# The MLP's first projection in 11 tiles instead of 12: gates and values of the last 64 units share one tile

## The chip, the cores and the metric

The kernel runs on one core of a Trainium2 chip. The core has a matrix engine (TensorE, PE in the rows, with its weight loads as PEld), three engines for elementwise work (VectorE or DVE, ScalarE or ACT, GpSimd or POOL), a queue that issues DMAs (SyncE or SP), an on-chip memory of 128 partitions and PSUM, eight banks of 128 partitions by 512 fp32 numbers into which TensorE writes. The metric is the device time of one execution in microseconds (us); lower is better. Before: 1258.32 us, the median of 3 runs (1258.1 to 1260.74).

## The reference, cut to what matters

A decoder block in fp32 on x of shape (4, 512, 256): causal self-attention with 16 heads, cross-attention with 16 heads of 16, and a network of two layers of local attention and a gated MLP. Each sub-block adds its result to x. The change touches the MLP alone, which runs for 2 layers and 4 batches, eight times:

```python
h = shift_token(x)                                   # half the channels moved one token on
h = (h - mean) / sqrt(var + 1e-05) * lg + lb
h = h @ w1 + b1                                      # (512, 256) @ (256, 1364)
a, g = jnp.split(h, 2, axis=-1)                      # values and gates, 682 each
h = a * jax.nn.gelu(g, approximate=False)
x = x + h @ w2 + b2                                  # (512, 682) @ (682, 256)
```

## The kernel before, in words

Every engine has its own list of instructions, written out in order, and waits on semaphores. The first half of the time is self-attention (a loop over 32 pairs of heads) and cross-attention. Then come eight steps, m = 0 to 7, one for a layer and a batch (layer m // 4, batch m % 4). A step has tokens to q, k, v (`qkv_tile`), rotation and norms, four pairs of heads of local attention (scores `Sa` and `Sb`, softmax, transposes `Ta` and `Tb`, weighted values `AV`), an output projection (`wo`), and the MLP: `stats`, `norm`, `apply`, `hnT` (the normed tokens transposed), the first projection `hid0` to `hid5` and the second `w20` and `w21`.

The steps overlap. Four strings (`STEP_PE`, `STEP_DVE`, `STEP_ACT`, `STEP_POOL`, lines 312 to 325) say in which order each engine goes through one cycle; `hid5@-1` there is the last tile of the MLP of the step before, `hT@2` the transposes of y for the step after the next. Items whose step doesn't exist (m over 7) drop out. The last items, from `closing` (line 376) on, are in an order of their own, with the MLP of step 7 at the very end.

The MLP's 682 hidden units are cut into NF = 6 tiles: five of FT = 114 and one of FL = 112. For a tile f TensorE makes first the gates (`w1g`) and then the values (`w1a`), each into a PSUM bank of its own, [units, 512 tokens], as a product of six matmuls: two halves of the 256 channels, and for each three terms, since weights and tokens are split into a rounded part and a rest (`w1_hi`, `w1_lo`, `hnT_hi`, `hnT_lo`) (`hidden_part`, line 1797; the instructions are recorded under line 1461 in the helper `product`). ScalarE applies GELU with the gate's bias to the gates and writes `gl` (`gates`, L950). VectorE adds the value's bias to the values, multiplies with `gl` and writes `hid` (`hidden`, L1388). The second projection (`second_part`, line 1810) takes for each half of the tokens 12 products of 256 columns, which TensorE runs as 24 instructions, with the units of a tile as the contracted dimension. It waits until VectorE has read the values of the last three tiles.

PSUM banks 2, 5, 6 and 7 (class "g") go round among q, k, v, the projections, the shifted half and the weighted values, in the order of TensorE's list (`turn`, line 395): a product waits until the bank's user four turns before has been read. In the trace all of these are called psum, both weight parts w, and q, k, v's weights wqkv.

Around the last tile TensorE's order is: transposes `Ta2`, `hid5`, `v3` (the last v tile of the next step), `hT`, `w20`. On ScalarE it is `hid4 Ta2 hid5`, then rounded weights (once), `hT` and the exponentials `eb3`. On VectorE `hid4 Ta2 hid5`, then `hT`.

Of the kernel before, what the change touches and what calls it, by code (L numbers as in the profile page):

```python
# [27 lines left out]
NF = 6  # L28
FT = -(-HID // NF)
FL = HID - FT * (NF - 1)  # L30
W = 128
# [50 lines left out]
def build(nc, a, out, x2_dram):  # L82

    with ExitStack() as ctx:
        def sem(name):
            return ctx.enter_context(nc.semaphore(name))

        def sbt(stack, name, shape, dt=F32):
            return stack.enter_context(nc.sbuf_tensor(name, shape, dt))
# [87 lines left out]
        w1_hi = sbt(ctx, "w1_hi", [P, E2, 2 * HID], F32R)  # L177
        w2 = sbt(ctx, "w2", [FT, NF, D])
        wo = sbt(ctx, "wo", [P, FPAIRS, D])
        lng = sbt(ctx, "lng", [P, DEPTH, E2])  # L180
        lnb = sbt(ctx, "lnb", [P, DEPTH, E2])
        b1 = sbt(ctx, "b1", [FT, DEPTH, 2, NF])
        b2 = sbt(ctx, "b2", [P, D])
# [11 lines left out]
        gl = sbt(ctx, "gl", [P, GELU_T, S])  # L195
        hid = sbt(ctx, "hid", [FT, NF, S])

# [56 lines left out]
        ld_shift = sem("ld_shift")  # L254
        w_hi, w_lo = sem("w_hi"), sem("w_lo")
        w1_hi_ok, w1_lo_ok = sem("w1_hi_ok"), sem("w1_lo_ok")
        hn_hi, hn_lo = sem("hn_hi"), sem("hn_lo")
# [141 lines left out]
        for what, *at in pe_order:  # L399
# [18 lines left out]
            if what == "w1":  # L418
                turn(("w1g", *at), "g")
                turn(("w1a", *at), "g")  # L420
            if what == "sh":
# [26 lines left out]
        def wait_read(eng, use):  # L448

            bank, n = use  # L450
            eng.wait_ge(read[bank], n + 1)
# [5 lines left out]
        def wait_early(eng):  # L457

            wait_full(eng, plan["KV", B - 1])
            wait_full(eng, plan["x1T", B - 1, 1])  # L460

        def frows(f):
            return FT if f < NF - 1 else FL

# [14 lines left out]
        def _(sp):  # L479
# [28 lines left out]
            def layer_w2(l):  # L508
                main = a["w2"][l, 0:FT * (NF - 1), :].rearrange("(k p) c -> p k c", p=FT)
                sp.dma_start(w2[:, 0:NF - 1, :], main).then_inc(ld_w2, 16)  # L510
                sp.dma_start(w2[0:FL, NF - 1, :], a["w2"][l, FT * (NF - 1):HID, :]).then_inc(ld_w2, 16)

# [90 lines left out]
        def _(pool):  # L603
# [67 lines left out]
            def rotate_k(m, t):  # L671
# [10 lines left out]
                pool.tensor_tensor(k3, k3, r, ALU.mult).then_inc(l_k, 1)  # L682

            def mlp_rstd(m):

                pool.wait_ge(f_mv, T * (m + 1))
                pool.tensor_scalar(rstd[:, 0, :], mv[:, 0, :, 1], LN_EPS, None, ALU.add).then_inc(f_eps, 1)
                pool.wait_ge(f_eps, m + 1)
                pool.tensor_tensor(rstd[:, 0, :], rstd[:, 0, :], neg_half[:, 0:T], ALU.pow).then_inc(f_rstd, 1)
# [53 lines left out]
        def _(act):  # L743
# [200 lines left out]
            def gates(m, f):  # L944
                use = plan["w1g", m, f]
                bank = wait_full(act, use)
                if f >= GELU_T:
                    wait_read(act, plan["w1a", m, f - GELU_T])
                rows = frows(f)
                act.activation(gl[0:rows, f % GELU_T, :], bank[0:rows, :], ACT.Gelu,  # L950
                               bias=b1[0:rows, m // B, 1, f:f + 1]).then_inc(read[use[0]], 1)

# [38 lines left out]
        def _(dve):  # L991
# [390 lines left out]
            def hidden(m, f):  # L1382

                use = plan["w1a", m, f]
                wait_read(dve, plan["w1g", m, f])
                bank = wait_full(dve, use)
                rows = frows(f)
                dve.scalar_tensor_tensor(hid[0:rows, f, :], bank[0:rows, :], b1[0:rows, m // B, 0, f:f + 1],  # L1388
                                         gl[0:rows, f % GELU_T, :], ALU.add, ALU.mult).then_inc(read[use[0]], 1)

# [64 lines left out]
        def _(pe):  # L1455
# [341 lines left out]
            def hidden_part(m, f):  # L1797
                if f == 0:
                    pe.wait_ge(hn_lo, E2 * (m + 1))
                    if m % B == 0:  # L1800
                        pe.wait_ge(w1_lo_ok, E2 * (m // B + 1))
                rows = frows(f)
                for what, lo in (("w1g", HID + f * FT), ("w1a", f * FT)):
                    use = plan[what, m, f]
                    bank = wait_free(pe, use)
                    product(bank[0:rows, :], [(w[:, e, lo:lo + rows], h[:, e, :]) for e in range(E2)
                                              for w, h in ((w1_hi, hnT_lo), (w1_lo, hnT_hi), (w1_hi, hnT_hi))])\
                        .then_inc(full[use[0]], 1)

            def second_part(m, tp):  # L1810
                for f in range(NF - 3, NF):
                    wait_read(pe, plan["w1a", m, f])
                if m % B == 0:
                    pe.wait_ge(ld_w2, 32 * (m // B + 1))
                use = plan["w2", m, tp]
                bank = wait_free(pe, use)
                for i in range(2):
                    t = 2 * tp + i
                    ins = product(bank[:, i * D:(i + 1) * D],
                                  [(hid[0:frows(f), f, t * P:(t + 1) * P], w2[0:frows(f), f, :]) for f in range(NF)])  # L1820
                ins.then_inc(full[use[0]], 1)
# [88 lines left out]
```

## Time and profile before

| | before |
|---|---|
| median of 3 runs | 1258.32 us (1258.1 to 1260.74) |
| the profiled execution | 1258.88 us |
| its span, first to last instruction | 1257.1 us |
| mean granted TensorE clock | 0.986 |
| TensorE busy | 1168.3 us (93%) |
| VectorE busy | 840.2 us (67%) |
| ScalarE busy | 686.9 us (55%) |
| GpSimd busy | 587.9 us (47%) |

The durations of TensorE's instructions overlap: one starts while the one before it still drains. Busy time is the time covered by at least one of them, and the time that an instruction adds to a row of them is the distance from start to start. A line of a chain of waits gives start, length and what ran, with the number of instructions; in it, the times follow each other without a gap. In the rows of a timeline, brackets give the idle time ahead of the instruction and what ended it.

### The profile page before, as it was taken

How to read it: one execution, taken by the hardware profiler on the slowest of the kernel's cores; microseconds unless marked ns; L12 is line 12 of the kernel's file. 1: busy time of each engine (PE TensorE's matmuls, PEld its weight loads, DVE VectorE, ACT ScalarE, POOL GpSimd, SP SyncE). 2: the span in 40 equal slices, each digit the busy share in tenths (PEclk: the TensorE clock that was granted, in tenths of full speed). 3: DMA queues.
4: the chain of work that ended last, by engine and by line, in shares of the span. 5: the costliest groups of instructions: out<-in, count | busy, mean ns of one | idle time of the engine just before them, and what ended most of it. 6: DMA issues, size and time to landing. Idle time of an engine off the chain costs nothing.

```text
span 1257.1 us, 20486 instructions
## 1 busy us (share of the span) xinstructions
PE 1168.3 (93%) x6672; PEld 893.2 (71%) x6672; DVE 840.2 (67%) x2443; ACT 686.9 (55%) x1696; POOL 587.9 (47%) x648
## 2 busy tenths in 40 slices
PE   5899999999999899986689999999999999999888
PEld 4677777777777666755467787777877778777666
DVE  7677777778777365588688657667675776755331
ACT  3667667577676034162366746647465565654721
POOL 2344454444544211147677556564655646563430
PEclk9899999999999999998799999999999999999999
DMA  7112122121223210014000000000001000010010
GB/s 226 44 42 76 35 50 72 38 50 34 51 51 109 77 34 1 1 59 159 1 2 1 1 1 18 1 2 1 1 18 45 28 2 1 2 64 4 1 51 17
DMA packets 31628, 46.11 MB, mean 37 GB/s; under 512 B 4572, under 2 KB 19632, under 8 KB 31536
## 3 DMA queue, kind: packets, MB, share of 16 engines
q1 hardware_dynamic: 31536, 44.98, 12.6%
q8 instruction: 45, 0.74, 0.3%
q14 instruction: 47, 0.39, 0.1%
HBM read 24.00 MB, written 4.19 MB: 22 GB/s over the span
## 4 chain that ended last, share of the span: by engine, by line
PE 53%; issue 20%; POOL 15%; DVE 7%; ACT 4%; DMA 0%; POOLq 0%; DVEq 0%; ACTq 0%
PE psum L1461 33%; POOL probs L625 13%; PE psum L1721 5%; PE psum L1770 4%; PE psum L1755 4%; PE psum L1737 4%; PE psum L1703 2%; ACT hnT_hi L941 1%; DVE stats L994 1%; ACT hnT L941 1%; POOL rn L669 1%; DVE ra L1276 1%; PE psum L1783 1%; DVE rb L1282 1%; DVE xn L1003 1%
## 5 line engine op out<-in xcount | busy, mean ns | idle before, releaser
L625 POOL TENSOR_TENSOR probs<-probs,rden 128x128 f32<-128x128 f32 (+3 forms) x256 | 177.5, 731 | 213.2 <-DVE rden L1055 213.2
L911 ACT ACTIVATE lp<-lp,lneg,rn 128x256 f32<-128x256 f32 (+1 forms) x256 | 143.8, 571 | 17.6 <-DVE lneg L1332 17.4
L780 ACT ACTIVATE probs<-probs,negmax 128x128 f32<-128x128 f32 (+3 forms) x256 | 140.6, 554 | 21.7 <-DVE negmax L1050 21.6
L1043 DVE CUSTOM_DVE_ANT_0 probs<-psum,causal 128x512 f32<-128x512 f32 (+3 forms) x256 | 110.1, 486 | 3.3 <-PE psum L1461 1.4
L669 POOL TENSOR_TENSOR rn<-ss,neg_half 128x8 f32<-128x8 f32 x64 | 107.0, 1671 | 3.8
L1320 DVE CUSTOM_DVE_ANT_0 lp<-psum,local 128x256 f32<-128x256 f32 (+1 forms) x256 | 84.0, 383 | 22.8 <-PE psum L1721 22.8
L660 POOL TENSOR_TENSOR lp<-lp,lrden 128x768 f32<-128x768 f32 x64 | 95.0, 1484 | 0.0
L1461 PE MATMUL psum<-q,k_rest 128*128 128x256 f32 (+2 forms) x256 | 88.9, 358 | 5.4 <-DVE rowmax L1043 3.1
L1527 PE MATMUL psum<-ident,probs 128*128 128x128 f32 x640 | 91.0, 274 | 1.7 <-POOL probs L625 1.6
L1461 PE MATMUL psum<-wqkv_hi,hT_lo 128*128 128x512 f32 x192 | 83.5, 435 | 4.4 <-DVE rb L1282 2.1
L657 POOL TENSOR_TENSOR lp<-lp,lrden 128x128 f32<-128x128 f32 x64 | 26.7, 418 | 128.1 <-DVE lrden L1337 128.1
L1461 PE MATMUL psum<-w,hid 114*128 114x256 f32 (+1 forms) x384 | 85.4, 379 | 1.1 <-DVE hid L1388 1.1
L665 POOL TENSOR_TENSOR ra<-ra,rb 128x512 f32<-128x512 f32 x32 | 41.0, 1280 | 93.0 <-DVE rb L1282 93.0
L1461 PE MATMUL psum<-hnT_lo,w_hi 128*114 128x512 f32 (+1 forms) x192 | 79.4, 413 | 3.5 <-DVE hnT_lo L1309 3.5
L898 ACT ACTIVATE sq<-psum 128x512 f32<-128x512 f32 x64 | 38.1, 598 | 80.0 <-PE psum L1461 73.4
L1388 DVE SCALAR_TENSOR_TENSOR hid<-psum,b,gl 114x512 f32<-114x512 f32 (+1 forms) x48 | 36.0, 750 | 67.3 <-PE psum L1461 53.9
L1461 PEld LDWEIGHTS psum<-w,hid 114*128 114x128 f32 (+1 forms) x384 | 72.3, 190 | 11.8 <-DVE hid L1388 1.5
L745 ACT ACTIVATE pT<-psum 128x512 f32<-128x512 f32 (+1 forms) x96 | 49.3, 515 | 57.2 <-PE psum L1527 57.2
L1721 PE MATMUL psum<-lkT,lqT 64*128 64x256 f32 (+1 forms) x512 | 67.8, 384 | 12.5 <-DVE lmax L1320 9.3
L1461 PE MATMUL psum<-q,k 128*128 128x256 f32 (+2 forms) x256 | 79.2, 327 | 0.0
L1527 PEld LDWEIGHTS psum<-ident,probs 128*128 128x128 f32 x640 | 74.3, 141 | 6.8 <-POOL probs L625 2.1
L1543 PE MATMUL psum<-pT,v 128*64 128x256 f32 (+3 forms) x512 | 76.0, 439 | 2.3 <-ACT pT L745 1.7
(166 smaller groups left out, 3064.4 us busy)
## 6 DMA issues: line engine op xcount, KB each, us to landing
k<-k_round SPq DMA_DIRECT2D x128, 128.0 KB, 2.4
x<-in_x SPq DMA_DIRECT2D x8, 512.0 KB, 6.0
aw<-in_w_quads SPq DMA_DIRECT2D x4, 768.0 KB, 5.1
w_raw<-in_w SPq DMA_DIRECT2D x2, 1364.0 KB, 6.6
ctxT<-in_ctxT SPq DMA_DIRECT2D x4, 512.0 KB, 3.5
x_scratch<-x SPq DMA_DIRECT2D x4, 512.0 KB, 3.7
x<-x_scratch SPq DMA_DIRECT2D x4, 512.0 KB, 5.4
wqkv_raw<-in_wqkv SPq DMA_DIRECT2D x1, 1536.0 KB, 10.0
```

The costliest lines, as they stand in the source:

```text
L625: ins = pool.tensor_tensor(pr, pr, rden[:, j % 2, h, i:i + 1].broadcast_to([P, TRI[i]]), ALU.mult)
L660: pool.tensor_tensor(pr, pr, r, ALU.mult).then_inc(l_prob, 1)
L669: pool.tensor_tensor(rn[:, m % 2, t, i, :], ss[:, i, :], neg_half[:, 0:FH], ALU.pow).then_inc(l_rn, 1)
L780: ins = act.activation(pr, pr, ACT.Exp, bias=negmax[:, j % 2, h, i:i + 1], scale=ADH ** -0.5, accum_out=den[:, j % 2, h, i:i + 1])
L911: ins = act.activation(pr, pr, ACT.Exp, bias=lneg[:, u % 2, h, w:w + 1], scale=rn[:, m % 2, w, 0, 2 * j + h:2 * j + h + 1], accum_out=lden ...
L1043: ins = dve.tensor_tensor_reduce(probs[:, j % 2, h, TRI_AT[i]:TRI_AT[i + 1]], bank[:, at:at + TRI[i]], causal[:, S - TRI[i]:S], 1.0, -3e38 ...
L1320: ins = dve.tensor_tensor_reduce(lp[:, u % 2, h, lo:hi], bank[:, at:at + hi - lo], local[:, LOC - (hi - lo):LOC], 1.0, -3e38, ALU.add, ALU ...
L1461: ins = mm(dst, lhsT, rhs, start=i == 0, stop=i == len(pairs) - 1, **kw)
L1527: ins = pe.transpose(bank[:, at:at + P], probs[:, j % 2, h, lo:lo + P], ident[:, :])
L1543: ins = mm(bank[rows, c * P:S], v[:, b % 2, c, cols], pT[:, h, KEYB_AT[c]:KEYB_AT[c] + KEYB[c]], start=c == 0, stop=c == T - 1)
L1721: ins = mm(pair[h][:, at:at + n].rearrange("p (w k) -> p w k", k=P), lqT[rows, c, d, :], keys[rows], start=True, stop=True)
L1737: ins = pe.transpose(bank[:, at:at + P], lp[:, u % 2, h, lo:lo + P], ident[:, :])
```

## The change

The hidden units are cut into five tiles of 124, 124, 124, 124 and 122 and a last one of 64. The last tile's gates and values are made together: one product of 128 rows in one bank, the gates in partitions 0 to 63, the values in 64 to 127. So there are 11 products of six matmuls in place of 12. ScalarE reads the lower half of the bank and writes GELU to the upper half of `gl`; VectorE waits for it on a semaphore of its own (`last_gate`), reads the values in the upper half of the bank and `gl` beside them, and writes the lower half of `hid`. It alone frees the bank.

On the host, w1's columns are put in the order of the tiles (gates, then values, for each), and w2's rows are laid out tile by tile, so that one DMA loads it in place of two. In the last tile the second projection contracts over all 128 partitions; w2's upper 64 rows there are zero, and GpSimd sets that tile of `hid` to zero once, ahead of the first MLP's `mlp_rstd`. The biases follow the same layout.

```diff
-FT = -(-HID // NF)
-FL = HID - FT * (NF - 1)
+FHALF = P // 2
+FROWS = (124, 124, 124, 124, 122, FHALF)
+FAT = [sum(FROWS[:f]) for f in range(NF + 1)]
...
             if what == "w1":
                 turn(("w1g", *at), "g")
-                turn(("w1a", *at), "g")
+                if at[1] < NF - 1:
+                    turn(("w1a", *at), "g")
+                else:
+                    plan["w1a", at[0], at[1]] = plan["w1g", at[0], at[1]]
...
             def layer_w2(l):
-                main = a["w2"][l, 0:FT * (NF - 1), :].rearrange("(k p) c -> p k c", p=FT)
-                sp.dma_start(w2[:, 0:NF - 1, :], main).then_inc(ld_w2, 16)
-                sp.dma_start(w2[0:FL, NF - 1, :], a["w2"][l, FT * (NF - 1):HID, :]).then_inc(ld_w2, 16)
+                sp.dma_start(w2[:, :, :], a["w2"][l]).then_inc(ld_w2, 16)
...
+            def zero_hidden():
+
+                wait_full(pool, plan["xw", B - 1, 1])
+                pool.memset(hid[:, NF - 1, :], 0.0).then_inc(hid_zero, 1)
+
             def mlp_rstd(m):
 
+                if m == 0:
+                    zero_hidden()
...
-                rows = frows(f)
-                act.activation(gl[0:rows, f % GELU_T, :], bank[0:rows, :], ACT.Gelu,
-                               bias=b1[0:rows, m // B, 1, f:f + 1]).then_inc(read[use[0]], 1)
+                rows = FROWS[f]
+                bias = b1[0:rows, m // B, 1, f:f + 1]
+                if f < NF - 1:
+                    act.activation(gl[0:rows, f % GELU_T, :], bank[0:rows, :], ACT.Gelu, bias=bias)\
+                        .then_inc(read[use[0]], 1)
+                else:
+                    act.activation(gl[FHALF:P, f % GELU_T, :], bank[0:FHALF, :], ACT.Gelu, bias=bias)\
+                        .then_inc(last_gate, 1)
...
-                wait_read(dve, plan["w1g", m, f])
-                bank = wait_full(dve, use)
-                rows = frows(f)
-                dve.scalar_tensor_tensor(hid[0:rows, f, :], bank[0:rows, :], b1[0:rows, m // B, 0, f:f + 1],
-                                         gl[0:rows, f % GELU_T, :], ALU.add, ALU.mult).then_inc(read[use[0]], 1)
+                rows = FROWS[f]
+                if f < NF - 1:
+                    wait_read(dve, plan["w1g", m, f])
+                    bank = wait_full(dve, use)
+                    at = slice(0, rows)
+                else:
+                    bank = wait_full(dve, use)
+                    dve.wait_ge(last_gate, m + 1)
+                    if m == 0:
+                        dve.wait_ge(hid_zero, 1)
+                    at = slice(FHALF, P)
+                dve.scalar_tensor_tensor(hid[0:rows, f, :], bank[at, :], b1[at, m // B, 0, f:f + 1],
+                                         gl[at, f % GELU_T, :], ALU.add, ALU.mult).then_inc(read[use[0]], 1)
...
-                rows = frows(f)
-                for what, lo in (("w1g", HID + f * FT), ("w1a", f * FT)):
+                for what in ("w1g", "w1a") if f < NF - 1 else ("w1g",):
+                    rows = FROWS[f] if f < NF - 1 else P
+                    lo = 2 * FAT[f] + (rows if what == "w1a" else 0)
...
-                                  [(hid[0:frows(f), f, t * P:(t + 1) * P], w2[0:frows(f), f, :]) for f in range(NF)])
+                                  [(hid[0:krows(f), f, t * P:(t + 1) * P], w2[0:krows(f), f, :]) for f in range(NF)])
```

On TensorE, in the full step that holds the last tile of MLP 4, this stood from the transposes ahead of the tile on (psum3 and psum4 take the transposed probabilities of `Ta2`, psum6 the gates, psum7 the values):

```order
L1737 MATMUL psum3<-ident,lp 128x128 x4
L1737 MATMUL psum4<-ident,lp 128x128 x3
L1461 MATMUL psum6<-hnT_lo,w1_hi 112x512
L1461 MATMUL psum6<-hnT_hi,w1_lo 112x512
L1461 MATMUL psum6<-hnT_hi,w1_hi 112x512
L1461 MATMUL psum6<-hnT_lo,w1_hi 112x512
L1461 MATMUL psum6<-hnT_hi,w1_lo 112x512
L1461 MATMUL psum6<-hnT_hi,w1_hi 112x512
L1461 MATMUL psum7<-hnT_lo,w1_hi 112x512
L1461 MATMUL psum7<-hnT_hi,w1_lo 112x512
L1461 MATMUL psum7<-hnT_hi,w1_hi 112x512
```

Now, at the same place (psum6 takes gates and values, psum7 the v tile):

```order
L1758 MATMUL psum3<-ident,lp 128x128 x4
L1758 MATMUL psum4<-ident,lp 128x128 x3
L1482 MATMUL psum6<-hnT_lo,w1_hi 128x512
L1482 MATMUL psum6<-hnT_hi,w1_lo 128x512
L1482 MATMUL psum6<-hnT_hi,w1_hi 128x512
L1482 MATMUL psum6<-hnT_lo,w1_hi 128x512
L1482 MATMUL psum6<-hnT_hi,w1_lo 128x512
L1482 MATMUL psum6<-hnT_hi,w1_hi 128x512
L1482 MATMUL psum7<-wqkv_hi,hT_lo 128x512
L1482 MATMUL psum7<-wqkv_lo,hT_hi 128x512
L1482 MATMUL psum7<-wqkv_hi,hT_hi 128x512
```

The second product of the tile is gone, and the v tile follows the first at once, in the bank that the values had.

On TensorE at the last tile of MLP 5, from the last matmul of the values (psum2) over the v tile (psum5) to the second projection (psum6), before:

```order
L1461 MATMUL psum2<-hnT_hi,w1_hi 112x512
L1461 MATMUL psum5<-wqkv_hi,hT_lo 128x512
L1461 MATMUL psum5<-wqkv_lo,hT_hi 128x512
L1461 MATMUL psum5<-wqkv_hi,hT_hi 128x512
L1461 MATMUL psum5<-wqkv_hi,hT_lo 128x512
L1461 MATMUL psum5<-wqkv_lo,hT_hi 128x512
L1461 MATMUL psum5<-wqkv_hi,hT_hi 128x512
L1461 MATMUL psum6<-w2,hid 128x256 x12
```

Now, from the last matmul of the shared tile (psum6) over the v tile (psum7) to the second projection (psum2):

```order
L1482 MATMUL psum6<-hnT_hi,w1_hi 128x512
L1482 MATMUL psum7<-wqkv_hi,hT_lo 128x512
L1482 MATMUL psum7<-wqkv_lo,hT_hi 128x512
L1482 MATMUL psum7<-wqkv_hi,hT_hi 128x512
L1482 MATMUL psum7<-wqkv_hi,hT_lo 128x512
L1482 MATMUL psum7<-wqkv_lo,hT_hi 128x512
L1482 MATMUL psum7<-wqkv_hi,hT_hi 128x512
L1482 MATMUL psum2<-w2,hid 128x256 x12
```

No transposes of y stand between the tile and the second projection here, before or after; the tile ahead is one product shorter.

On TensorE at the last tile of MLP 6, from the last matmul of its gates (psum5) over the values (psum6) to the transposes of `Tb2` and the weighted values of the pair, before:

```order
L1461 MATMUL psum5<-hnT_hi,w1_hi 112x512
L1461 MATMUL psum6<-hnT_lo,w1_hi 112x512
L1461 MATMUL psum6<-hnT_hi,w1_lo 112x512
L1461 MATMUL psum6<-hnT_hi,w1_hi 112x512
L1461 MATMUL psum6<-hnT_lo,w1_hi 112x512
L1461 MATMUL psum6<-hnT_hi,w1_lo 112x512
L1461 MATMUL psum6<-hnT_hi,w1_hi 112x512
L1737 MATMUL psum3<-ident,lp 128x128 x4
L1737 MATMUL psum4<-ident,lp 128x128 x3
L1755 MATMUL psum7<-lpT,lv 64x256 x6
L1755 MATMUL psum7<-lpT,lv 64x128 x2
```

Now, from the fourth matmul of the shared tile (psum7) on:

```order
L1482 MATMUL psum7<-hnT_lo,w1_hi 128x512
L1482 MATMUL psum7<-hnT_hi,w1_lo 128x512
L1482 MATMUL psum7<-hnT_hi,w1_hi 128x512
L1758 MATMUL psum3<-ident,lp 128x128 x4
L1758 MATMUL psum4<-ident,lp 128x128 x3
L1776 MATMUL psum2<-lpT,lv 64x256 x6
L1776 MATMUL psum2<-lpT,lv 64x128 x2
```

The transposes and weighted values follow the first product, where the values' six matmuls stood between.

## Rows read from the trace of the kernel before

**Rows 1.** Page, busy time, share of the span and instructions.

```profile
PE 1168.3 (93%) x6672; PEld 893.2 (71%) x6672; DVE 840.2 (67%) x2443; ACT 686.9 (55%) x1696; POOL 587.9 (47%) x648
```

**Rows 2.** Stretches: length, busy by engine (instructions), granted clock, DMA share, GB/s.

```profile
core 0: us, PE busy (x) PEld busy (x) DVE busy (x) ACT busy (x) POOL busy (x), PEclk, DMA share, GB/s
...
920.00:980.00 60.00, 59.38 (x349) 45.41 (x348) 39.61 (x122) 35.27 (x79) 32.41 (x32) 1.00 0.10 33
```

**Rows 3.** Chain of work, a full step: start, length, what.

```profile
913.21 6.91 PE psum L1770 x32
...
960.57 4.17 PE psum L1461 x18
...
965.61 5.19 PE psum L1461 x24
...
978.33 7.96 PE psum L1461 x36
```

**Rows 4.** Weight loads by shape, 620 to 1258 us: busy, mean ns, idle before.

```profile
L1461 PEld LDWEIGHTS psum<-wqkv_hi,hT_hi 128*128 128x128 f32 x158 | 29.6, 188 | 6.8
L1461 PEld LDWEIGHTS psum<-hnT_hi,w_hi 128*114 128x114 f32 x160 | 28.9, 180 | 9.2
```

**Rows 5.** Timelines, last tile of MLP 3: start, length, instruction.

```profile
962.00 0.69 ACT L950 ACTIVATE gl<-psum,b 112x512 f32<-112x512 f32 x1 [0.84 <-PE psum L1461]
...
958.42 0.68 DVE L1282 TENSOR_TENSOR rb<-psum,tab 128x512 f32<-128x512 f32 x1
...
963.47 0.75 DVE L1388 SCALAR_TENSOR_TENSOR hid<-psum,b,gl 112x512 f32<-112x512 f32 x1 [1.55 <-PE psum L1461]
...
965.45 1.89 PE L1461 MATMUL psum<-w,hid 114*128 114x256 f32 x8
```

**Rows 6.** Timelines of ScalarE and TensorE, last tile of MLP 5.

```profile
1121.48 0.69 ACT L950 ACTIVATE gl<-psum,b 112x512 f32<-112x512 f32 x1 [0.84 <-PE psum L1461]
...
1124.07 5.35 PE L1461 MATMUL psum<-w,hid 114*128 114x256 f32 x24
```

**Rows 7.** Chain of work behind the last tile of MLP 6.

```profile
1187.26 0.69 ACT gl L950
...
1200.44 4.51 PE psum L1770 x20
```

**Rows 8.** Timeline of TensorE at four waits; in brackets the idle time.

```profile
579.50 0.55 PE L1461 MATMUL psum<-wqkv_hi,hT_lo 128*128 128x512 f32 x1 [2.08 <-DVE rb L1282]
...
1192.13 1.73 PE L1755 MATMUL psum<-lpT,lv 128*64 128x256 f32 x16 [2.75 <-ACT lpT L745]
...
1195.23 0.95 PE L1737 MATMUL psum<-ident,lp 128*128 128x128 f32 x7 [0.45 <-ACT lpT L745]
...
1222.30 0.77 PE L1461 MATMUL psum<-hnT_lo,w_hi 128*114 128x512 f32 x1 [3.52 <-DVE hnT_lo L1309]
```

**Rows 9.** Chain of work, end of the kernel.

```profile
1222.30 19.72 PE psum L1461 x72
...
1242.11 0.76 DVE hid L1388
...
1243.12 10.62 PE psum L1461 x48
```

**Rows 10.** By line: count, duration ns min/median/max, first and last start, shape.

```profile
L1032 DVE TENSOR_TENSOR k_rest<-psum,k_round x32: 649/673/683, 20.3 to 395.6; 64x512 fp32r<-64x512 f32 x32
...
L1025 DVE TENSOR_TENSOR q<-psum,q x32: 683/685/687, 21.7 to 399.1; 64x512 fp32r<-64x512 f32 x32
...
L605 POOL MEMSET k_rest<- x1: 952/952/952, 0.8 to 0.8; 128x1024 f32 x1
```

**Rows 11.** Timeline of GpSimd ahead of the first MLP.

```profile
683.50 0.23 POOL L687 TENSOR_SCALAR rstd<-mv 128x4 f32<-128x4 f32 x1 [2.67 <-DVE mv L1365]
```

**Rows 12.** Stretches, as rows 2; the granted clock is the third from last.

```profile
580.00:582.00 2.00, 2.00 (x7) 1.42 (x6) 1.97 (x5) 0.60 (x1) 1.90 (x2) 0.50 1.00 366
582.00:584.00 2.00, 1.04 (x5) 0.64 (x3) 1.97 (x4) 1.08 (x2) 1.90 (x3) 0.70 1.03 423
...
1226.00:1228.00 2.00, 2.00 (x7) 1.43 (x6) 0.13 (x1) 0.00 (x0) 0.00 (x0) 0.50 0.00 0
```

More of the change, by code:

```diff
@@ L28 @@
 NF = 6
-FT = -(-HID // NF)
-FL = HID - FT * (NF - 1)
+FHALF = P // 2
+FROWS = (124, 124, 124, 124, 122, FHALF)
+FAT = [sum(FROWS[:f]) for f in range(NF + 1)]
+assert FAT[NF] == HID
 W = 128
@@ L177, in build @@
         w1_hi = sbt(ctx, "w1_hi", [P, E2, 2 * HID], F32R)
-        w2 = sbt(ctx, "w2", [FT, NF, D])
+        w2 = sbt(ctx, "w2", [P, NF, D])
         wo = sbt(ctx, "wo", [P, FPAIRS, D])
@@ L181, in build @@
         lnb = sbt(ctx, "lnb", [P, DEPTH, E2])
-        b1 = sbt(ctx, "b1", [FT, DEPTH, 2, NF])
+        b1 = sbt(ctx, "b1", [P, DEPTH, 2, NF])
         b2 = sbt(ctx, "b2", [P, D])
@@ L195, in build @@
         gl = sbt(ctx, "gl", [P, GELU_T, S])
-        hid = sbt(ctx, "hid", [FT, NF, S])
+        hid = sbt(ctx, "hid", [P, NF, S])
         loT = sbt(ctx, "loT", [P, FPAIRS, S])
@@ L255, in build @@
         w_hi, w_lo = sem("w_hi"), sem("w_lo")
+        hid_zero, last_gate = sem("hid_zero"), sem("last_gate")
         w1_hi_ok, w1_lo_ok = sem("w1_hi_ok"), sem("w1_lo_ok")
@@ L460, in wait_early @@
             wait_full(eng, plan["x1T", B - 1, 1])
-        def frows(f):
-            return FT if f < NF - 1 else FL
         def wqkv_part(l, c):
@@ L1808, in hidden_part, with krows @@
                         .then_inc(full[use[0]], 1)
+            def krows(f):
+                return FROWS[f] if f < NF - 1 else P
             def second_part(m, tp):
@@ L1813, in second_part @@
                 if m % B == 0:
-                    pe.wait_ge(ld_w2, 32 * (m // B + 1))
+                    pe.wait_ge(ld_w2, 16 * (m // B + 1))
                 use = plan["w2", m, tp]
@@ L1880, in hidden_rows, with columns_by_tiles, by_hidden_tiles @@
         parts = np.asarray(w).reshape(DEPTH, 2, HID)
-        filled = np.concatenate([parts, np.zeros((DEPTH, 2, FT * NF - HID), parts.dtype)], 2)
-        return filled.reshape(DEPTH, 2, NF, FT).transpose(0, 3, 1, 2)
+        rows = np.zeros((DEPTH, P, 2, NF), parts.dtype)
+        for f in range(NF):
+            for k in range(2):
+                at = FHALF if f == NF - 1 and k == 0 else 0
+                rows[:, at:at + FROWS[f], k, f] = parts[:, k, FAT[f]:FAT[f + 1]]
+        return rows
+    def columns_by_tiles(w):
+        parts = [np.asarray(w)[..., k * HID + FAT[f]:k * HID + FAT[f + 1]] for f in range(NF) for k in (1, 0)]
+        return np.concatenate(parts, -1)
+    def by_hidden_tiles(w):
+        tiles = np.zeros((DEPTH, P, NF, D), np.asarray(w).dtype)
+        for f in range(NF):
+            tiles[:, 0:FROWS[f], f, :] = np.asarray(w)[:, FAT[f]:FAT[f + 1], :]
+        return tiles
     arrays = {
@@ L1894 @@
         "wqkv": L0_ffn_wqkv, "q_scale": L0_ffn_q_scale, "k_scale": L0_ffn_k_scale, "wo": L0_ffn_wo,
-        "ln_g": by_rows(L0_ffn_ln_g), "ln_b": by_rows(L0_ffn_ln_b), "w1": L0_ffn_w1, "b1": hidden_rows(L0_ffn_b1),
-        "w2": L0_ffn_w2, "b2": L0_ffn_b2,
+        "ln_g": by_rows(L0_ffn_ln_g), "ln_b": by_rows(L0_ffn_ln_b), "w1": columns_by_tiles(L0_ffn_w1), "b1": hidden_rows(L0_ffn_b1),
+        "w2": by_hidden_tiles(L0_ffn_w2), "b2": L0_ffn_b2,
     }
```

## The prediction, made before the changed kernel ran

> **What bounds the kernel now.** I read the busy shares of the page first, then the stretches, then the chain of work that ended last. TensorE is busy 93% of the span [rows 1]. In the stretch from 920 to 980 us, in the middle of the two layers, TensorE is busy 59.4 of 60 us at full clock, while VectorE has 39.6, ScalarE 35.3 and GpSimd 32.4 us [rows 2]. The chain of one step, which spans some 80 us, is nearly all TensorE [rows 3]: its first projection, its second, the projections to q, k, v. So in these steps an instruction less on TensorE is time off the end, at the pace at which TensorE issues, which is not an instruction's duration, since those overlap: 18 products of 512 columns take 4.17 us in the chain [rows 3], 232 ns each. One product of six is 1.39 us.
>
> **What the change removes.** Eight MLPs (two layers, four batches, numbered 0 to 7) each lose one product of six, 48 matmuls in all. If all lay on the path that would be 8 x 1.39 = 11.1 us. What is left must not run slower. The stationary operand grows from 114 to 122 or 124 columns and in the last tile from 112 to 128; such a load takes 180 ns at 114 columns and 188 at 128 [rows 4], both under the 232 ns of the matmul beside it. The q, k, v products have 128 columns and keep the pace: 36 instructions in 7.96 us are 12 of them and 24 of the second projection, which alone take 5.19, leaving 2.77 for 12, 231 ns each [rows 3]. The second projection gets 124, 122 or 128 rows of hid in place of 114 or 112. The attention's output projection has 128 rows and the same 256 columns: 32 in 6.91 us, 216 ns, as the 24 in 5.19 [rows 3]. I take zero for both; the bound from these rows is below 0.01 us per product either way.
>
> **What is added, and the new wait.** Before, the gates of the last tile were worked on by ScalarE while TensorE made the values, and VectorE's product followed the values. Now both halves end together, and what follows is in series: gate, then the product, then the second projection. In a full step the gate starts at 962.00 and takes 0.69; VectorE starts 0.04 after it and takes 0.75 [rows 5]; TensorE starts 0.26 after VectorE's end, as in the closing (1242.11 + 0.76 to 1243.12) [rows 9]. That makes 963.74. The second projection began at 965.45 and would now come 1.39 earlier, at 964.06: 0.32 us to spare. What covers the wait is the v tile and the transposes of y that TensorE does in between. Five MLPs (0 to 4) have this cover: 5 x 1.39 = 6.95 us.
>
> MLP 5 has no transposes of y behind it, since batch 8 does not exist. Its gate starts at 1121.48: 1121.48 + 0.69 + 0.04 + 0.75 + 0.26 = 1123.22, against 1124.07 before [rows 6]. Gain 0.85 us, a wait of some 0.54 takes the rest.
>
> MLP 6: the chain leaves TensorE at the end of the first product of its last tile, goes to the gate at 1187.26, a table load, the exponentials of the last attention pair and an eviction, and gets back to TensorE at 1192.13 [rows 7, 8]. The product that goes is behind that point, and TensorE waits 2.75 us there already [rows 8]. Gain 0; the idle gap grows to 2.75 + 1.39 = 4.14 us.
>
> MLP 7, the last, has nothing between its tile and the second projection. The tile ended at 1222.30 + 19.72 = 1242.02; now 1.39 earlier, 1240.63. Then 0.03 + 0.69 + 0.04 + 0.76 + 0.25 gives 1242.40, against 1243.12 [rows 9]. Gain 0.72 us.
>
> Together 6.95 + 0.85 + 0 + 0.72 = 8.52 us.
>
> What else moves. The last tile takes one PSUM bank in place of two, so the v tile behind it gets the bank of the k tile before instead of that of the gates; VectorE let go of that bank with the operation at 958.42, 0.68 long [rows 5], while the v tile starts near 962: hidden, with 2.8 us to spare. From there each use of the four banks comes no later than before. The memset of the hidden tile is at most the 0.95 us of one twice as long, once, in GpSimd's queue ahead of the first MLP's statistics, where GpSimd sat idle for 2.67 us [rows 10, 11]: hidden; if it were not, 0.95 once. The one weight transfer in place of two has the same weights in longer pieces, and no row shows TensorE waiting for it. The gate's output and VectorE's output now go to other partitions than the input's. The nearest rows are VectorE's: 64x512 across halves 685 ns, 64x512 in place 673 [rows 10]. So I take the old durations; for ScalarE across halves no row exists. The low bound is those same durations, since 112 and 114 rows took equally long; the high bound I set at twice these durations, 1.44 us more for the two together, and take the low end, which the row across halves is next to.
>
> **The clock.** TensorE's granted clock has two levels here, 2.4 and 1.2 GHz (1.00 and 0.50 in the rows). After an idle gap of 2.08 us before 579.50 and one of 3.52 us before 1222.30 it stood at 0.50; after one of 2.75 us before 1192.13 TensorE went on at its full pace [rows 8, 12]. The gap at MLP 6 now becomes 4.14 us, longer than all three. I expect the clock to fall there to 1.2 GHz. The Trainium skill, TensorE: Matmul & The Clock Gate, section Why this matters for your kernels, tells to avoid long idle gaps between bursts of matmuls because the clock goes back to half rate; that speaks against this change at this one place. By that rule the price below is paid, by a clock that stays up the sum is 8.52.
>
> The price from rows: from 1222.30, 72 matmuls took 19.72 us instead of 72 x 0.232 = 16.7 [rows 9], a loss of 3.0 with the clock low to 1228 at least [rows 12]. The low stretch at 580 was shorter: 0.50 and 0.70 in two stretches of 2 us are 2.0 + 1.2 = 3.2 us [rows 12], and a little ahead of 580, say 3.4; half of that, 1.7, is lost where TensorE has work throughout. Behind the gap TensorE has work up to 1204.95 [rows 7] but for a wait of 0.45 [rows 8], which would take up as much. So 1.25 to 2.6 us; I take the middle, 1.9.
>
> **Sum.** 8.52 - 1.9 = 6.6 us. The profiled execution took 1258.88 (its span of 1257.1 and 1.8 around it), so 1252.3. The median of the runs shown is 0.56 lower: 1251.7.
>
> **Rivals.**
> (a) The clock stays up at MLP 6: for it, the 2.75 us gap that kept it; against it, the shorter one of 2.08 us that lost it. 8.5 us gained, 1249.8.
> (b) All eight products count, because the chain at MLP 6 and 7 loosens: against it is that the gate there hangs on the first product alone. 11.1 us, 1247.2.
> (c) The clock falls a second time, at the last second projection: TensorE's wait there grows from 1.10 to some 1.78 us, close to the 2.08 that lost it. 48 matmuls in 10.62 us follow [rows 9], so 1.7 to 3.0 us more: 1253.4 to 1254.7.
> (d) Slower: operations from one half of the partitions to the other run twice as long on ScalarE and VectorE. An extra x is then waited for by TensorE: five times x - 0.32, once x at MLP 5, about half of it (the gate) at MLP 6 and x at MLP 7, so 7.5x - 1.6, against 8.5 - 1.9. It turns slower from x = 1.1. At x = 1.44 it is 9.2 - 6.6 = 2.6 us slower: 1260.9. VectorE's row across halves speaks against it.
> (e) That the change doesn't do what it says: 48 matmuls fewer stand in TensorE's list of instructions, so no chance is kept for it.
>
> **How the numbers follow.** Forecast 0.60, its own range 1250.8 to 1253.0 from the bounds of the clock's price. (a) 0.21, (b) 0.04, (c) 0.13, (d) 0.02. The range 1249.0 to 1254.3 holds the forecast, (a) and most of (c), and leaves out (b), (d) and a part of (c), with what small errors add about 0.15. A difference under 0.2% (2.5 us) can't be told from none here. All cases but (d) are over 2.5 us faster; allowing for a mistake common to all, faster 0.96, within 0.2% 0.02, slower 0.02.
>
> **What would show it.** In the profile after: 528 matmuls of the first projection in place of 576, at an unchanged pace (18 in 4.2 us become 12 in 2.8, last tile and v); the second projection of MLPs 0 to 4 starting without idle time, that of MLP 5 after a wait of about 0.5 us on the hidden tile, that of MLP 7 after about 1.8; every full step 1.39 us shorter; an idle gap of about 4.1 us before the values of the last pair but one, followed by a granted clock of 0.5 for 3 to 7 us; gate and product at 0.69 and 0.75 in the last tile too. I am wrong if the gate across halves is longer, if a full step keeps its length, or if the gap keeps the clock up.

## The result, and the profile after

The changed kernel takes 1252.5 us (median of five executions, 1250.5 to 1253.7), against 1258.5 us for the kernel before on the same chip (five executions, 1258.1 to 1260.7). The ratio is 0.9947, with a 95% interval of 0.9932 to 0.9961: 4.9 to 8.6 us less. The forecast was 1251.7. The profiled execution took 1250.48 (span 1248.7) against 1258.88 (span 1257.1), 8.40 less. Part of that is no effect of the change: the first gate of the first MLP starts at 700.50 instead of 701.66 us, though the engines' work ahead of it is the same in both but for the memset and the layout of the weights. In a second profile of each (e7 and e8 below) it starts at 701.90 and 701.89. In twelve profiles of this study that start lies between 700.0 and 702.7.

So I measure from that first gate (of MLP 0) to the first matmul of the last MLP's second projection. The rest behind that point, some 14 us, is alike in both.

| | profile one | profile two |
|---|---|---|
| before | 701.66 to 1243.12: 541.46 | 541.50 |
| after | 700.50 to 1234.68: 534.18 | 534.20 |

Two profiles of one kernel agree within 0.04 us in this interval, and the change is worth 7.28 us in it. It is called "the interval" below.

The page after, the counterpart of [rows 1]: busy time of each engine, share of the span, instructions.

```profile
PE 1157.8 (93%) x6624; PEld 888.6 (71%) x6624; DVE 840.0 (67%) x2443; ACT 686.4 (55%) x1696; POOL 588.9 (47%) x649
```

TensorE has the 48 matmuls less, GpSimd one instruction more (the memset). TensorE's busy time fell by 10.5 us and the span by 8.4, so its share is 93% as before.

The stretch of [rows 2] again, in the columns named there:

```profile
920.00:980.00 60.00, 59.38 (x351) 47.08 (x348) 42.01 (x116) 37.24 (x83) 34.27 (x32) 1.00 0.07 24
```

TensorE is busy 59.38 us as before. The others have more in these 60 us (VectorE 42.0 for 39.6, ScalarE 37.2 for 35.3), since more of a step now fits in.

The last tile of MLP 3, from the timelines of the three engines, the counterpart of [rows 5] (start, length, instruction, in brackets the idle time ahead):

```profile
956.28 0.68 ACT L963 ACTIVATE gl<-psum,b 64x512 f32<-64x512 f32 x1 [0.85 <-PE psum L1482]
...
957.08 0.76 DVE L1409 SCALAR_TENSOR_TENSOR hid<-psum,b,gl 64x512 f32<-64x512 f32 x1 [0.88 <-ACT gl L963]
...
958.35 3.84 PE L1482 MATMUL psum<-w,hid 124*128 124x256 f32 x17
```

Gate and product run one behind the other now. The hidden tile is ready at 957.08 + 0.76 + 0.26 = 958.10, and the second projection starts at 958.35 with no idle time in brackets: 0.25 us to spare, where 0.32 was worked out. The difference is VectorE's start: 0.12 us behind the end of the gate here (956.28 + 0.68 to 957.08), and 0.04 was taken. Working across the halves of the partitions has no price that can be seen. Here are the eight of each, and two kinds of weight loads, by shape between 620 and 1249 us (busy us, mean ns of one, idle ahead), the counterpart of [rows 4]:

```profile
L1482 PEld LDWEIGHTS psum<-hnT_hi,w_hi 128*124 128x124 f32 x128 | 24.1, 189 | 6.2
L1482 PEld LDWEIGHTS psum<-hnT_hi,w_hi 128*128 128x128 f32 x16 | 3.0, 187 | 0.7
L963 ACT ACTIVATE gl<-psum,b 64x512 f32<-64x512 f32 x8 | 5.4, 681 | 8.0 <-PE psum L1482 8.0
L1409 DVE SCALAR_TENSOR_TENSOR hid<-psum,b,gl 64x512 f32<-64x512 f32 x8 | 6.0, 755 | 7.5 <-ACT gl L963 6.6 <-PE psum L1482 0.9
```

681 and 755 ns stand against 0.69 and 0.75 us in place, on 112 partitions [rows 5]. The weight loads at 189 and 187 ns stay under the pace of 232.

TensorE's waits after, from its timeline, the counterpart of [rows 8] and the end of [rows 6]:

```profile
1114.74 5.43 PE L1482 MATMUL psum<-w,hid 124*128 124x256 f32 x24 [0.46 <-DVE hid L1409]
...
1182.88 3.25 PE L1776 MATMUL psum<-lpT,lv 128*64 128x256 f32 x16 [4.14 <-ACT lpT L753]
...
1187.56 0.95 PE L1758 MATMUL psum<-ident,lp 128*128 128x128 f32 x7 [0.45 <-ACT lpT L753]
```

MLP 5 waits 0.46 us on its hidden tile. At MLP 6 the idle gap grew from 2.75 to 4.14 us, and behind it the 16 matmuls of the attention pair take 3.25 us instead of 1.73: the clock. The stretches there and at the end (columns as in [rows 2]; the granted clock is the third from last):

```profile
1184.00:1188.00 4.00, 3.55 (x24) 2.25 (x22) 0.56 (x1) 1.08 (x2) 4.00 (x3) 0.72 0.07 23
...
1214.00:1220.00 6.00, 5.36 (x13) 4.12 (x14) 0.59 (x1) 1.55 (x2) 0.00 (x0) 0.50 0.01 3
```

And the end of the chain of work, the counterpart of [rows 9] (start, length, what):

```profile
1214.64 18.23 PE psum L1482 x66
1232.89 0.69 ACT gl L963
1233.67 0.77 DVE hid L1409
1234.68 10.63 PE psum L1482 x48
```

72 matmuls in 19.72 us became 66 in 18.23, which is 1.49 less. From the end of the tile to the second projection it was 1.10 us and is 1.81, since the gate now stands in series: that puts 0.71 back and leaves 0.78. The 48 matmuls behind took 10.63 us, as before, so the wait of 1.83 us here did not cost the clock in this execution.

The terms, each as a difference between the first gate and the point named:

| Term | predicted | measured |
|---|---|---|
| MLPs 0 to 4 (first gate to second projection of MLP 4, 343.53 to 336.18) | 6.95 | 7.35 |
| MLP 5 (to its second projection) | 0.85 | 0.82 |
| MLP 6 (to its gate) | 0 | -0.09 |
| clock behind the gap at MLP 6 (gate to second projection, 20.10 to 21.68) | -1.9 | -1.58 |
| MLP 7 (35.76 to 34.98) | 0.72 | 0.78 |
| sum | 6.62 | 7.28 |

The 0.4 us too much in the first term is at one step. Steps without weight copies went from 79.74 to 78.33 us (1.41 less), that of MLP 2 from 81.49 to 79.82 (1.67 less). TensorE's waits on VectorE between 700 and 1120 us (in all, times, longest) in the profile of before:

```profile
PE psum L1703 <- DVE hT_lo L1264: 1.4, 1, 1.4
```

and of after, up to 1110 us:

```profile
PE psum L1724 <- DVE hT_lo L1277: 1.1, 1, 1.1
```

There VectorE's first two copies of the rests of the next layer's weights took 2.73 instead of 3.11 us, and the one wait on VectorE in that range is 0.27 shorter. Why these copies were quicker I did not find out. It is no scatter between executions: the wait was 1.39 us in all three profiles with the layout of before (before, e4, e7), 1.11 to 1.12 in the six with that of after (after, e2, e5, e8, e9, e10), 1.52 in e1, and 1.86 and 1.84 in e3 and e6.

### The profile page after: what moved, and what is told of

It reads as the page before. It is cut to its first block, busy times and chain, and to the rows that moved or that the text cites. A ratio compares the mean times of both kernels' runs of the same rounds, so it can differ in the third digit from the quotient of the medians.

```text
span 1248.7 us, 20389 instructions
## 1 busy us (share of the span) xinstructions
PE 1157.8 (93%) x6624; PEld 888.6 (71%) x6624; DVE 840.0 (67%) x2443; ACT 686.4 (55%) x1696; POOL 588.9 (47%) x649
## 4 chain that ended last, share of the span: by engine, by line
PE 53%; issue 20%; POOL 15%; DVE 7%; ACT 4%; DMA 0%; POOLq 0%; DVEq 0%; ACTq 0%
PE psum L1482 32%; POOL probs L626 13%; PE psum L1742 5%; PE psum L1791 4%; PE psum L1776 4%; PE psum L1758 4%; PE psum L1724 2%; ACT hnT_hi L949 1%; DVE stats L1007 1%; ACT hnT L949 1%; POOL rn L670 1%; DVE ra L1289 1%; PE psum L1804 1%; DVE rb L1295 1%; DVE xn L1016 1%
## 5 line engine op out<-in xcount | busy, mean ns | idle before, releaser
L1482 PE MATMUL psum<-w,hid 124*128 124x256 f32 (+2 forms) x384 | 85.5, 379 | 2.3 <-DVE hid L1409 2.3
L1482 PEld LDWEIGHTS psum<-w,hid 124*128 124x128 f32 (+2 forms) x384 | 72.2, 190 | 13.3 <-issue 3.1
L1409 DVE SCALAR_TENSOR_TENSOR hid<-psum,b,gl 124x512 f32<-124x512 f32 (+2 forms) x48 | 36.1, 752 | 61.7 <-PE psum L1482 41.7
L1482 PE MATMUL psum<-wqkv_hi,hT_hi 128*128 128x512 f32 x192 | 77.0, 401 | 0.0
```

Of the source, the lines that this page charges most:

```text
L1482: ins = mm(dst, lhsT, rhs, start=i == 0, stop=i == len(pairs) - 1, **kw)
```

## The experiments

Expectations are quoted as they stood before each run. All ratios are against the kernel before on the same chip. The theory: TensorE's issue pace sets the time of MLPs 0 to 5 and 7, a gap at MLP 6 costs the clock. The rivals: the gain comes from the layout (longer tiles, one weight transfer less), not from the matmuls; the clock has no part in it.

**e1: the matmuls put back, the layout kept.** The product of the v tile is done twice in steps 2 to 7, so that six matmuls come back behind the last tile of MLPs 0 to 5. Nothing else is changed.

```diff
-                product(bank[:, :], [(h[:, e, rows], w[:, e, cols]) for e in range(E2)
-                                     for h, w in ((hT_lo, wqkv_hi), (hT_hi, wqkv_lo), (hT_hi, wqkv_hi))])\
-                    .then_inc(full[use[0]], 1)
+                for _ in range(2 if what == "v" and t == T - 1 and m in range(2, STEPS) else 1):
+                    ins = product(bank[:, :], [(h[:, e, rows], w[:, e, cols]) for e in range(E2)
+                                               for h, w in ((hT_lo, wqkv_hi), (hT_hi, wqkv_lo), (hT_hi, wqkv_hi))])
+                ins.then_inc(full[use[0]], 1)
```

> The changed kernel, with the last v tile of steps 2 to 7 made twice into its bank, so that MLPs 0 to 5 have twelve products of six matmuls between the same points again and all else stays as changed. Theory (TensorE's issue pace is what was saved): 5 x 1.39 for MLPs 0 to 4 come back, and at MLP 5 1.39 less the wait of 0.46 us that the product now fills: 7.9 us more than the changed kernel's 1252.5, 1260.4. Rival (the gain comes from the layout, the single weight transfer or scatter in the first half): 1252.5 to 1254.

Measured: 1258.81 us (eleven executions) against 1258.74, ratio 1.0002 [0.9993, 1.0011]. From the first gate to the second projection of MLP 5 it takes 422.30 us; before has 422.41, after 414.24. Chain of work of e1 at MLP 5 (start, length, what):

```profile
1117.53 0.76 PE psum L1759 x7
1118.29 9.37 PE psum L1482 x42
```

The wait on the hidden tile at MLP 5 is gone: last tile, the doubled v and the second projection run on as 18 x 0.232 + 24 x 0.216 = 9.36 us. TensorE's wait on VectorE at MLP 2 is back too:

```profile
PE psum L1725 <- DVE hT_lo L1277: 1.5, 1, 1.5
```

So the gain of MLPs 0 to 5 is the matmuls': with the new layout and the old number of matmuls, 0.11 us of the 8.17 is left. The gap at MLP 6, which e1 leaves as in after, cost the clock here also, as TensorE's timeline shows:

```profile
1190.40 3.25 PE L1777 MATMUL psum<-lpT,lv 128*64 128x256 f32 x16 [4.14 <-ACT lpT L753]
```

The median came 1.6 us under the expectation; the interval, at 541.79, is 7.61 longer than after's.

**e2: the gap at MLP 6 filled.** Eight throwaway matmuls write to the bank that the attention pair's own first matmul starts afresh; they stand in TensorE's list where it would wait for ScalarE.

```diff
+            def filler(bank, n):
+                for _ in range(n):
+                    mm(bank[:, 0:D], ident[0:P, :], w2[0:P, 0, :], start=True, stop=True)
...
+                if u == UNITS - 2:
+                    filler(wait_free(pe, plan["O", u]), 8)
```

> The changed kernel, with 8 matmuls of 256 columns in fp32 (16 instructions, 3.5 us) put into TensorE's idle gap of 4.14 us at MLP 6, into the bank that the product behind overwrites. Theory (the clock fell there and cost 1.6 us in the profiled execution, more in others): granted clock 1.00 after the gap, the weighted values behind it in 1.7 us instead of 3.25, and 1.5 to 3 us less than 1252.5: about 1250.5. Rival (the clock is lost for other reasons, or its loss is taken up by waits behind it): 1252.5.

Measured: 1249.15 us (six executions, 1248.0 to 1251.1), ratio 0.9924 [0.9913, 0.9936]. TensorE's timeline in e2:

```profile
1185.04 1.73 PE L1782 MATMUL psum<-lpT,lv 128*64 128x256 f32 x16 [0.68 <-ACT lpT L753]
```

0.68 us of the gap is left and the 16 matmuls take 1.73 us again, 1.5 less than in after. The interval is 531.56, 2.6 shorter than after's. The other 1.0 of it lies at the end, where nothing was changed: the 66 matmuls took 17.19 us for 18.23, behind the same wait of 3.52 us. The clock came back sooner: worked out from the granted clock of stretches of 2 us, an estimate, it was low for some 3.4 us there in e2 and 6.8 in after. Nothing in e2 was aimed at this place, and its median, 3.35 us under after's, is more than the filling explains.

**e3: the shared tile as the fourth of six.** Gates and values in series now have two tiles behind them, and the last tile is an ordinary one, whose values follow its gates.

```diff
-FROWS = (124, 124, 124, 124, 122, FHALF)
+SH = 3
+FROWS = (124, 124, 124, FHALF, 124, 122)
...
-                if f < NF - 1:
+                if f != SH:
```

(and `NF - 1` to `SH` at the other places that single out the shared tile)

> The changed kernel with the shared tile as the fourth of the six instead of the last; the last is of 122 with two products. Theory (the last tile's gate, then product, then second projection were exposed at MLPs 5 and 7, and the removed product at MLP 6 lay in TensorE's idle time): all eight products of 1.39 us count, 11.1 us under before's 1258.5: 1247.4, with TensorE's gap at MLP 6 back at 2.75 us; if the clock stays up there it is at this value, if it falls 1 to 2 us above. Rival (the shared tile's chain costs as much wherever it stands, through banks held longer): 1251 to 1252.5.

Measured: 1247.03 us (four executions, 1246.4 to 1248.0), ratio 0.9906 [0.9892, 0.9921]. The waits at MLPs 5 and 7 shrank as expected (at the end 1.12 us, for 1.83 in after), but the gap at MLP 6 was 3.19 us and not 2.75. Timeline of TensorE in e3:

```profile
1182.57 0.65 PE L1777 MATMUL psum<-lpT,lv 128*64 128x256 f32 x4 [3.19 <-ACT lpT L754]
```

and of ScalarE:

```profile
1175.34 1.28 ACT L961 ACT_TABLE_LOAD   x1
1176.63 0.69 ACT L961 ACTIVATE gl<-psum,b 124x512 f32<-124x512 f32 x1
1177.22 0.59 ACT L754 ACTIVATE lpT<-psum 128x512 f32<-128x512 f32 x1
1177.70 0.69 ACT L961 ACTIVATE gl<-psum,b 122x512 f32<-122x512 f32 x1
```

The last gate's product was done at 1177.26, but ScalarE, held up since its table load, got to it only at 1177.70: 0.44 us later than TensorE allowed, and the gap is that much longer. The clock fell there (the stretch from 1184 to 1188 us has 0.64). My expectation had taken the gate as bound by TensorE alone. By it, a clock that falls puts the time 1 to 2 us above 1247.4, so the median of 1247.03 agrees with its number and not with its account. In the interval e3 takes 530.91, 10.55 less than before. TensorE's wait on VectorE at MLP 2 was 0.47 us longer than in before; the expectation had nothing on it.

**e4 and e5: the clock taken out of both kernels.** The kernel before with five and seven such matmuls, at the gap of MLP 6 and ahead of the last first projection, and the kernel after with eight and seven. If the clock is the only loss, e4 minus e5 is the change's value without it, 8.52 us by the prediction.

```diff
+                if u == UNITS - 2:
+                    filler(wait_free(pe, plan["O", u]), 5)
...
+                    if m == STEPS - 1:
+                        filler(wait_free(pe, plan["w1g", m, f]), 7)
```

(this is e4, with `filler` as in e2; e5 has 8 in place of 5; the seven stand ahead of the last MLP's first tile)

> The kernel before, with 5 fp32 matmuls of 256 columns in TensorE's gap of 2.75 us at MLP 6 and 7 in the gap of 3.52 us ahead of the last MLP's first projection. Theory (low clock after idle gaps): the last first projection's 72 matmuls in 16.7 instead of 19.7 us, 3.0 us less than 1258.5, and up to 2 more if the gap at MLP 6 loses the clock in the usual execution: 1253.5 to 1255.5. Rival (the clock doesn't follow idle time): 1258.5.

> The changed kernel with both fillings: 8 fp32 matmuls of 256 columns in TensorE's gap at MLP 6 and 7 in the gap ahead of the last MLP's first projection. Theory (low clock costs 2.9 us at the end, as in the kernel before with fillings, and some 3 at MLP 6): 2.9 us under the changed kernel with the first filling alone (1249.15): 1246.3. Against the kernel before with both fillings (1255.84) this is the change without its effect on the clock: 8.5 us by the sum of the prediction, 1247.3. Rival (the two low stretches overlap in what they cost): 1248 to 1249.

Measured: e4 1255.84 us (eleven), ratio 0.998 [0.9971, 0.9989]; e5 1247.0 us (four, 1245.4 to 1248.7), ratio 0.9902 [0.9885, 0.9918]. The interval is 538.71 in e4 and 529.97 in e5, 8.74 apart. The chain of e4 at the end:

```profile
1222.56 16.97 PE psum L1461 x72
```

19.72 us became 16.97: the low clock had cost 2.75 there, in the kernel before too. The median of 1255.84 lies 0.34 above the range expected: only the last first projection got shorter, since the clock had held at MLP 6 in before. The chain of e5 at the end, with its stretch behind (columns as in [rows 2]):

```profile
1213.89 15.55 PE psum L1482 x66
...
1231.27 12.32 PE psum L1482 x48
```

```profile
1231.00:1235.00 4.00, 3.73 (x10) 3.02 (x11) 0.01 (x1) 0.00 (x0) 0.00 (x0) 0.57 0.00 0
```

In this execution the clock did fall at the last second projection, behind the wait of 1.83 us, and its 48 matmuls took 12.32 us, not 10.63. That is rival (c) of the prediction: the mechanism exists. It showed neither in the two profiles of after nor in e1, e2 and e10, which have the same wait (1.83 to 1.86 us). The median of e5 is 0.7 above the expected 1246.3.

**e6: the fourth tile shared, and both gaps filled.** e3 with six and seven such matmuls.

```diff
+                if u == UNITS - 2:
+                    filler(wait_free(pe, plan["O", u]), 6)
...
+                    if m == STEPS - 1:
+                        filler(wait_free(pe, plan["w1g", m, f]), 7)
```

> The shared tile as the fourth of six, with 6 fp32 matmuls of 256 columns in the gap at MLP 6 (3.19 us in its profile) and 7 in the one ahead of the last MLP's first projection. Theory: the variant without fillings took 1247.03 and had the clock low for 3.4 us at either place, some 1.5 us each: 1244 to 1244.5. Rival (with the shared tile moved, the rest is set by ScalarE and the low clock is hidden): 1246 to 1247.

Measured: 1245.19 us (four executions, 1243.8 to 1246.3), ratio 0.9888 [0.9872, 0.9905], the fastest version here, 13 us under the kernel before. Chain of e6:

```profile
1213.82 15.58 PE psum L1483 x66
1229.49 0.76 DVE hid L1410
1230.50 10.64 PE psum L1483 x48
```

Full pace at both places, and only VectorE's product ahead of the last second projection. The interval is 528.10, 13.4 shorter than before's. Against e4, the kernel before with the clock filled in the same way (538.71), it is 10.61 less, of the 11.1 that eight products are worth. The median is 0.7 above the expectation and 0.8 under the rival's lower end; the times alone don't separate the two, and the full pace in the trace is what speaks for the theory.

**e7 and e8: the kernels before and after once more, unchanged.** For whether the clock falls at MLP 6 in each.

> The kernel before, once more, with a profile. If its idle gap of 2.75 us at MLP 6 can lose the clock in one execution and keep it in another, with the first half shifted by a microsecond, part of the runs carry the low clock there already; if it never does, the gap's growth to 4.14 us alone brought it. From the gaps seen so far (2.08 us lost it, 2.75 kept it in one profile): as likely low as not. The time of the eight steps behind the first gate should be the same 541.5 us within 0.3 if the clock stays up, 1.5 to 3 more if not.

> The changed kernel, once more, with a profile: from the first gate to the last second projection it took 534.2 us, with the clock low for 3.4 us at MLP 6 and 6.8 ahead of the last MLP. Theory: the clock is low behind the 4.14 us gap again, for 3.4 or 6.8 us; 534.2 or up to 1.5 more. Rival (the fall there was this execution's alone): clock 1.00 there and 532.6.

Measured: e7 1259.17, e8 1251.86 (one execution each). TensorE's timelines, e7:

```profile
1192.37 1.74 PE L1755 MATMUL psum<-lpT,lv 128*64 128x256 f32 x16 [2.75 <-ACT lpT L745]
```

and e8:

```profile
1184.26 3.26 PE L1776 MATMUL psum<-lpT,lv 128*64 128x256 f32 x16 [4.14 <-ACT lpT L753]
```

The same again: 2.75 us kept the clock in two profiles of two, 4.14 lost it in three of three (e1 counted). These are few, and other gaps show that one program can go either way. TensorE idles for 2.08 us ahead of 579.50 in before, where the clock fell to 0.50, and for the same 2.08 us ahead of 577.41 in e7, where it stayed at 1.00 for the 5 us behind; 2.02 us ahead of 665.60 in before kept it, and 2.02 us ahead of 664.51 in e7 lost it. So whether 2.75 us keeps the clock in every execution of the kernel before is not shown.

**e9: a third filling, ahead of the last second projection.** e5 with three more matmuls.

```diff
+                if m == STEPS - 1 and tp == 0:
+                    filler(wait_free(pe, plan["w2", m, tp]), 3)
```

> The changed kernel with both fillings and a third, 3 fp32 matmuls of 256 columns (1.3 us) in TensorE's wait of 1.83 us ahead of the last second projection, into the bank that it writes. With two fillings the profiled execution had the clock low for 3.4 us there and the 48 matmuls took 12.3 instead of 10.6 us. Theory (that fall followed the wait of 1.83 us): 10.6 us, clock 1.00, and 0.5 to 1.7 us under the 1247.0 with two fillings, by how many executions lose it: 1246.2. Rival (the fall has another cause, or it was rare): 1247.0.

Measured: 1246.33 us (five executions, 1244.9 to 1248.2), ratio 0.9908 [0.9894, 0.9921]. TensorE's timeline in e9 shows the short wait and the full pace:

```profile
1230.88 5.43 PE L1482 MATMUL psum<-w,hid 124*128 124x256 f32 x24 [0.54 <-DVE hid L1409]
```

The clock held in the profile. Against e5 (0.9902) no difference can be measured; one that only some executions pay would be within the scatter of both. The theory and the rival of a rare fall are not told apart.

**e10: the gap at MLP 6 brought back to about its old length.** After with three such matmuls there, not eight.

```diff
+                if u == UNITS - 2:
+                    filler(wait_free(pe, plan["O", u]), 3)
```

> The changed kernel with 3 fp32 matmuls of 256 columns, 1.3 us, in the gap at MLP 6 alone: about what the removed product took there, so the idle time is some 2.8 us as in the kernel before. Theory (removing that product gained nothing and lost the clock): the clock stays up as in both profiles of before, the weighted values behind the gap take 1.7 us and the time is 1.5 to 2.5 us under 1252.5: 1250.5. Rival (a product put back costs its 1.3 to 1.4 us, or the clock falls at 2.8 us as well): 1252.5 to 1253.9.

Measured: 1250.65 us (five executions, 1249.1 to 1252.4), ratio 0.9943 [0.993, 0.9957]. TensorE's timeline:

```profile
1183.14 3.25 PE L1782 MATMUL psum<-lpT,lv 128*64 128x256 f32 x16 [2.84 <-ACT lpT L753]
```

The idle time is 2.84 us, 0.09 more than in before, and the clock fell all the same, with the whole price of 1.5 us. So the median is near the expected 1250.5, but the account behind that number failed. The interval is 534.11, for 534.18 in after: 1.3 us of matmuls put back into this gap cost nothing, and by themselves bring nothing. The length of the idle time alone does not separate 2.75 from 2.84. The ratio's interval overlaps that of after; how often the clock falls at such a gap stays open.

## Why the prediction was right, point by point

- **TensorE bounds the middle of the kernel, and a product is worth its issue pace.** Shown: steps without weight copies are 1.41 us shorter, for 1.39, and e1, which puts the matmuls back, takes 422.30 us up to MLP 5, for 422.41 in before.
- **The series of gate, product and second projection is covered by 0.32 us in MLPs 0 to 4.** Seen: 0.25 to spare and no idle time. The series itself was taken 0.05 to 0.08 too short, since VectorE starts 0.09 to 0.12 behind the gate and not 0.04. At MLP 5 the loss against a full product was 1.39 - 0.82 = 0.57 for 0.54 (the idle time in brackets, 0.46, counts from the end of the last matmul); at MLP 7 the wait was 1.83 for 1.78.
- **No price for working across the halves of the partitions.** Seen, 681 and 755 ns; rival (d) is out. This was the choice of the low end of a wide bound, by VectorE's row, and it held for ScalarE too.
- **Weight loads of 124 and 128 columns, more rows in the second projection, the memset, the bank of v: nothing.** The loads take 187 to 189 ns, 24 matmuls of the second projection still take 5.19 us where TensorE has not waited, and no new wait appears between 700 and 1110 us.
- **MLP 6 gives nothing and loses the clock.** The gap was 4.14 us as worked out. The clock's price was the mis-sized term: 1.9 taken, 1.5 to 1.6 measured; it lies within 1.25 to 2.6, under the middle that I took. In e1 the same gap cost 2.2. Filling the gap (e2) gives the 1.5 back at the place. Rival (a) is out for this gap in the profiles taken. The reason that I gave, longer than gaps that lost the clock, is weak: e10 lost it at 2.84, and gaps of 2.08 and 2.02 us went either way in before and e7. That the clock fell was in part luck for the forecast, and with rival (a) the time would have been 1249.8, still within the range of 1249.0 to 1254.3.
- **Rival (b), 11.1 us,** is out: the gate at MLP 6 moved with TensorE's work ahead of it and the product behind bought nothing.
- **Rival (c)** was not in either profile of after but was in e5's, so it can hit some executions. It is a risk of single executions, and no cost of every one.
- **The sum.** 6.62 worked out, 7.28 in the interval, 4.9 to 8.6 by the ratio. The medians of five executions are 6.0 apart. The forecast's own range of 1250.8 to 1253.0 is wider than the clock's bounds make it: 1258.32 less 8.52 plus 1.25 or 2.6 is 1251.05 to 1252.4, and the rest has no working. The 0.66 between 6.62 and 7.28 are 0.40 at MLPs 0 to 4 (of it 0.27 a shorter wait of TensorE on VectorE's weight copies, cause open) and 0.32 of the clock, less 0.06 at the rest. Without the clock, 8.52 was worked out, and e4 minus e5 gives 8.74, with e5's own fall of the clock behind the end of the interval.

## What to carry to other kernels

Price a removed matmul at the engine's issue pace, not at its duration, and go through its instances one by one: where TensorE already waits behind it, the product buys only a longer gap, and the matmuls behind a gap can run at half the clock (1.5 us here). When a merge puts two engines in series, give the merged tile other tiles behind it rather than nothing (e3, e6). Where TensorE must idle for some microseconds ahead of a burst, throwaway matmuls into a bank that is about to be overwritten kept the clock up, in all ten places where they left less than 1 us idle (e2, e4, e5, e6, e9); the three of e10, which left 2.84 us, did not. They were worth 1.5 us at one gap and 2.75 at another, more together than half of what the change itself brought.

## What the runs showed of the hardware that was not expected

- The idle time ahead does not by itself decide whether the clock falls. In the last two MLPs it was kept behind 2.75 us (before, e7) and 1.83 to 1.86 us (after, e1, e2, e8, e10), and lost behind 4.14 (after, e1, e8), 3.52 (in all eight that had it), 3.19 (e3), 2.84 (e10), and 1.83 once (e5). Three gaps ahead of the first MLP, alike in all twelve profiles, went either way: 2.08 us near 579 lost it in ten and kept it in two (e2, e7), 2.02 us near 665 kept it in eleven and lost it in one (e7), and behind 3.22 us near 598 it stayed at 1.00 for 5 us in four (e4, e5, e6, e8) and fell within 2 us of the burst's start in the other eight. What decides it stays open.
- The same idle time has different prices. The price goes with how long the clock stays low, and that differs between executions: at MLP 6 some 3.4 us in after and 6.8 in e1, estimates from the granted clock of stretches of 2 us. Behind 4.14 us at MLP 6 the clock cost 1.5 us in after and e8, and 2.2 in e1, where the transposes behind the 16 matmuls ran low as well (four in 1.06 us for 0.60, seven in 1.20 for 0.95). Behind 3.52 us the 66 matmuls took 18.21 to 18.23 us in three profiles (after, e8, e10) and 17.15 to 17.19 in three others (e1, e2, e3), where 15.55 to 15.63 is full pace: 2.6 or 1.6 us.
- The first 700 us, the same work in all twelve profiles but for the memset and the layout of the weights, varied by 1.3 us to either side, nearly as much as the clock term here. An interval inside the trace, repeated within 0.04 us, told effects apart that the times of whole executions did not.
